# A two-layer transformer kernel with routed experts: token places in two pieces, bf16 ranks, biases joined to the shared sums, maxima split on 128 partitions, down weights quantized later

## The chip, the cores and the metric

The kernel runs on one core of a Trainium2 chip. The metric is the device time of one execution in microseconds (us). A profiled execution is another execution of the same program, recorded by the hardware profiler. In what follows PE is TensorE, DVE is VectorE, ACT is ScalarE, POOL is GpSimd and SP is SyncE, which here does nothing but issue DMAs. L913 is line 913 of the kernel before.

## What is computed

Eight batches (turns) of 512 tokens with 128 features go through two layers, in fp32 unless said otherwise:

```python
xn = layernorm(x)                       # x: (8, 512, 128)
x = x + attn0(xn) + ffn0(xn)            # 16 heads of 8; ffn0: gate, up, down with
                                        # FP4 quantize+dequantize (blocks of 16) of inputs and weights
xn = layernorm(x)
x = x + attn1(xn) + moe(xn)             # attn1 with biases
# moe: logits = relu(xf @ Wr1 + br1) @ Wr2 + br2; top 2 of 8 experts
# out = silu(xf @ Ws1 + bs1) @ Ws2 + bs2                      (shared expert)
# for each e: out += w[:, e] * (silu(xf @ We1[e] + be1[e]) @ We2[e] + be2[e])
```

The softmax of both attentions is taken with the maximum of each row of scores subtracted.

## The kernel before

All of it is written out by hand, engine by engine: five instruction streams (`block.sync`, `gpsimd`, `scalar`, `vector`, `tensor`), each in a fixed order, with semaphores between them. PSUM is divided into three rings. `ring` has two banks and carries every single product or transpose; `sums` (`acc`) has two banks for accumulations; `mx` has two double banks for scores. The order in which names take banks is written in `ring_uses`. An engine that is to reuse a bank waits for the reader of the bank's last content, so a late reader on DVE or ACT holds PE.

Turn `it` has these stages, seen from PE:

- **Scores of layer 0.** For slots k = 1 to 15, four score products (`scores`, L1329) for 4 heads by 128 keys, two exponentials of 128x1024 on ACT (L702), and eight weighted sums (L1321). Beside it DVE normalizes the next batch, quantizes the hidden FFN values (`hidden`), splits q and k of the next batch into three bf16 parts (`split_qk`, L849 to L853; the third part is a POOL subtraction, `third_part`, L527) and quantizes the tokens (`quantize_x`).
- **Scores of layer 1** of the batch before, again 16 slots. In each slot PE also makes two score tiles for the maxima of layer 0 of the next batch (`tile_maxima`, in `ring`; in turn 0 a pair in `mx`), which DVE reduces with a maximum (L917 or L913). Into the slots are set the projection of attention 0, the second normalization, the router, the q and k products of layer 1, and the ranks of the tokens among those that chose the same expert (`ranks`, L1386 to L1390: fp32 products of 0/1 matrices). DVE's `places` turns the ranks into row numbers and POOL's `sort_tokens` scatters the tokens with eight indirect DMAs and loads them back sorted. POOL's order is fixed: `third_part(1, it)`, then `sort_tokens(it)`.
- **The middle.** The shared expert (`shared_hidden`, `shared_out`), the output biases weighted by the router (`output_biases`, in a bank of their own, "mb"), the projection of attention 1, ten places for pairs of maxima, and the gate and up products.
- **The tiles.** 15 tiles of 128 sorted tokens, with expert weights fetched by indirect DMAs, and among them the remaining maxima of layer 0 and all 32 pairs of layer 1 (L913). At tile 4 the row maxima of layer 0 are transposed on PE (`max_rows`), and DVE splits the 16x512 result into two bf16 parts (`split_rows`, L929 and L931), which SP copies into the q stacks as two extra rows. The row maxima of layer 1 follow in the first slots of the next turn; in the last turn at tile 13.

Before turn 0 there is a start: loads, the first normalization, quantization of the FP4 weights in three pieces (gate, up, down; `quantize_weights`), the first q and k split, its stores to DRAM and loads back as stacks (SP, L416 to L430), and the 32 pairs of maxima of batch 0.

DVE's slot order in the second stage before the change (slot_maxima first in each slot) is:

```python
if k == 3: add_projection(0, part, it, it); dve.drain(); norm_stats(1, it)
if k == 4: norm_apply(1, it)
if k == 5 and it > 0: add_experts(it - 1)
if k == 10: split_qk(1, part, it, it); places(part, it)
if k == 11: gate_difference(part, it); sums_out(1, part, it, it - 1, 0)   # the latter if it > 0
```

## Time and profile before

| what | value |
|---|---|
| median of 3 runs | 1478.62 us (1476.63 to 1479.34) |
| the profiled execution | 1480.99 us, of which the span from first to last instruction is 1479.2 us |
| PE matmul busy | 1287.3 us (87%) |
| PE weight load busy | 609.3 us (41%) |
| DVE busy | 1074.9 us (73%) |
| ACT busy | 788.0 us (53%) |
| POOL busy | 401.7 us (27%) |
| mean granted TensorE clock | 0.948 of full |

Turns 1 to 6 are alike, and each takes about 171 to 172 us. The busy shares are averages over stages with different limits, so the stages are read one by one. In a timeline a row is: start in us, length in us, engine, line, operation, what it writes and reads, count, and in brackets the idle time of the engine just before and what ended it. An engine's pieces that follow each other closely are merged.

### The profile page before, as it was taken

The page shows a single profiled execution, that of the slowest core. Times are in us where ns is not written, and L with a number is a line of the kernel's source. Part 1 is how long each engine was busy: PE and PEld are TensorE (multiplying, and loading weights), DVE is VectorE, ACT ScalarE, POOL GpSimd, SP SyncE. Part 2 cuts the span into 40 slices and gives each one's busy share as a digit, 9 for nine tenths or more (in the row PEclk, how much of TensorE's full clock was granted, in tenths as well). Part 3 has the DMA queues.
Part 4 walks back from the last instruction along what each step waited for, and adds up shares of the span by engine and source line. Part 5 has one row for each costly group of instructions (what it writes and reads, how often), then busy time and mean ns, then how long its engine had stood idle before and what let it go on. Part 6 is the DMA issues. An engine that isn't in the chain of part 4 may idle for free.

```text
span 1479.2 us, 22025 instructions
## 1 busy us (share of the span) xinstructions
PE 1287.3 (87%) x7829; PEld 609.3 (41%) x7829; DVE 1074.9 (73%) x1907; ACT 788.0 (53%) x1279; POOL 401.7 (27%) x459
## 2 busy tenths in 40 slices
PE   1578789989999889998899899998899988999886
PEld 1113365334633256233553346332563336433641
DVE  8876789677985689766895779856896679824641
ACT  1145235754477534864357544776348643687355
POOL 6001333114231222314231233313223142303331
PEclk8669599999999999999999999999999999999998
DMA  3303373317514364226533275143642264203730
GB/s 111 100 9 109 119 219 106 99 54 219 161 47 127 96 183 144 86 64 190 150 97 104 65 200 168 40 128 96 192 134 92 58 198 144 90 5 104 223 100 15
DMA packets 120734, 171.76 MB, mean 116 GB/s; under 512 B 18153, under 2 KB 98354, under 8 KB 120626
## 3 DMA queue, kind: packets, MB, share of 16 engines
q0 software_dynamic: 27168, 90.44, 20.2%
q1 hardware_dynamic: 92514, 79.38, 18.3%
q8 instruction: 63, 1.03, 0.3%
q10 hardware_dynamic: 944, 0.54, 0.1%
q14 instruction: 45, 0.37, 0.1%
HBM read 116.88 MB, written 52.89 MB: 115 GB/s over the span
## 4 chain that ended last, share of the span: by engine, by line
PE 53%; DVE 28%; ACT 11%; issue 3%; DVEq 3%; DMA 2%; POOL 0%; ACTq 0%; POOLq 0%
DVE nm L913 19%; PE sums L1321 11%; PE mx L1329 11%; ACT ex L702 9%; PE ring L1211 8%; PE mx L1280 4%; PE ring L1410 3%; PE ring L1217 3%; PE sums L1422 3%; PE ring L1206 3%; PE ring L1280 2%; PE sums L1377 2%; PE ring L1259 2%; PE ring L1399 1%; DVE qk_f L851 1%
## 5 line engine op out<-in xcount | busy, mean ns | idle before, releaser
L702 ACT ACTIVATE ex<-mx 128x1024 f32<-128x1024 f32 x512 | 496.0, 1028 | 178.6 <-PE mx L1329 177.2
L913 DVE TENSOR_REDUCE nm<-mx 128x2 f32<-128x1024 f32 x422 | 490.2, 1215 | 68.1 <-PE mx L1280 68.1
L1329 PE MATMUL mx<-qs,ks 128*128 128x512 bf16 (+1 forms) x1024 | 287.6, 391 | 29.4 <-ACT ex L702 14.9
L715 ACT ACTIVATE ex<-ring,wx_sb 128x128 f32<-128x128 f32 x480 | 136.8, 368 | 222.6 <-PE ring L1410 222.6
L1280 PE MATMUL mx<-ks,qs 64*128 64x512 bf16 x844 | 162.6, 406 | 57.2 <-DVE nm L913 55.5
L1329 PEld LDWEIGHTS mx<-qs,ks 128*128 128x128 bf16 (+1 forms) x1024 | 80.2, 99 | 252.5 <-ACT ex L702 170.8
L552 POOL DMA_INDIRECT wx_sb<-wx,wx_row x120 | 114.6, 955 | 255.0 <-PE sums L1422 240.4
L917 DVE TENSOR_REDUCE nm<-ring 128x1 f32<-128x512 f32 x180 | 115.8, 685 | 62.7 <-PE ring L1280 61.6
L1410 PE MATMUL ring<-xsT,wx_sb 128*128 128x128 f32 x960 | 135.9, 285 | 8.5 <-ACT xsT L656 5.4
L1321 PE MATMUL sums<-ex,vs 128*18 128x512 f32 x1024 | 137.6, 610 | 0.0
L1422 PE MATMUL sums<-wx_sb,ex 128*128 128x128 f32 x960 | 135.6, 284 | 0.0
L1410 PEld LDWEIGHTS ring<-xsT,wx_sb 128*128 128x128 f32 x960 | 118.2, 194 | 25.2 <-issue 22.5
L1422 PEld LDWEIGHTS sums<-wx_sb,ex 128*128 128x128 f32 x960 | 117.0, 191 | 27.1 <-issue 25.9
L527 POOL TENSOR_TENSOR parts<-qk_f,parts 128x512 bf16<-128x512 f32 x32 | 36.3, 1152 | 234.0 <-DVE parts L853 234.0
L1280 PEld LDWEIGHTS mx<-ks,qs 64*128 64x128 bf16 x844 | 37.2, 94 | 151.8 <-DVE nm L913 69.7
L509 POOL TENSOR_TENSOR rstd<-veps,minus_half 128x4 f32<-128x4 f32 x16 | 17.7, 1103 | 260.3 <-DVE veps L835 260.2
L570 POOL DMA_INDIRECT x_sorted<-xn,slot x64 | 62.2, 971 | 63.4 <-DMA x_sorted<-xn,slot 35.4
L600 POOL DMA_INDIRECT xs<-o_sorted,slot x64 | 65.3, 1020 | 35.6 <-DMA xs<-o_sorted,slot 20.4
L1321 PE MATMUL sums<-ex,vs1b 128*18 128x512 f32 x512 | 70.8, 626 | 0.6 <-ACT ex L702 0.6
L1321 PE MATMUL sums<-ex,vs1a 128*18 128x512 f32 x512 | 70.8, 626 | 0.0
L560 POOL DMA_DIRECT2D o_sorted<-xs x32 | 26.1, 814 | 145.4 <-ACT xs L724 107.0
L936 DVE COPY work<-sums 128x512 f32<-128x512 f32 x32 | 22.0, 688 | 55.0 <-PE sums L1321 55.0
(191 smaller groups left out, 1403.0 us busy)
## 6 DMA issues: line engine op xcount, KB each, us to landing
scratch<-parts SPq DMA_DIRECT2D x64, 384.0 KB
ks<-scratch SPq DMA_DIRECT2D x256, 64.0 KB, 2.3
qs<-scratch SPq DMA_DIRECT2D x256, 64.0 KB, 2.2
scratch<-parts SPq DMA_DIRECT2D x32, 256.0 KB
xs<-x_sorted POOLq DMA_DIRECT2D x24, 256.0 KB, 7.5
o_sorted<-xs POOLq DMA_DIRECT2D x24, 256.0 KB, 2.8
rest<-parts SPq DMA_DIRECT2D x32, 128.0 KB
x_sb<-x SPq DMA_DIRECT2D x8, 256.0 KB, 3.3
```

The costliest lines, as they stand in the source:

```text
L552: pool.indirect_dma_start(wx_sb[n % NW][:, :], None, wx, bass.IndirectOffsetOnAxis(ap=wx_row[:, i:i + 1], axis=0)).then_inc(wx_in[n % NW], 16)
L600: pool.indirect_dma_start(moe[:, n, t, :], None, o_sorted, bass.IndirectOffsetOnAxis(ap=slot[it % 2][:, n, t:t + 1], axis=0)).then_inc(moe ...
L702: act.activation(ex[:, ex_buffer(l, b, k), 2 * i:2 * i + 2, :], mx[bank][:, :, :], ACT.Exp, scale=SCALE).then_inc(mx_free[bank], 1)
L715: last = act.activation(ex[:, free_buffer(it, "tiles"), c, i % TG * P:i % TG * P + P], bank[:, c * P:(c + 1) * P], ACT.Silu, bias=wx_sb[n ...
L913: dve.tensor_reduce(nm[l][:, t, h:h + 2], mx[bank][:, :, :], AX.X, ALU.max, negate=True).then_inc(mx_free[bank], 1)
L917: dve.tensor_reduce(nm[0][:, t, h:h + 1], bank[:, :], AX.X, ALU.max, negate=True).then_inc(free, 1)
L1211: pe.matmul(bank[0:rows, 0:width], lhsT, rhs, start=True, stop=True).then_inc(full, 1)
L1280: return pe.matmul(bank, qs[l][r, h, t * P:(t + 1) * P], ks[l][r, h, :], start=True, stop=True)
L1321: last = pe.matmul(acc[bank][32 * j:32 * j + 2 * VW, :], values[:, start:start + 2 * VW], ex[:, ex_buffer(l, b, k), j, :], start=q == 0 an ...
L1329: return pe.matmul(bank, ks[l][r, h, s * P:(s + 1) * P], qs[l][r, h, :], start=True, stop=True)
L1410: last = pe.matmul(bank[:, c * P:(c + 1) * P], wx_sb[n % NW][:, c * P:(c + 1) * P], xsT[:, i // TG % 2, i % TG * P:i % TG * P + P], start= ...
L1422: last = pe.matmul(acc[bank][:, i % TG * P:i % TG * P + P], ex[:, free_buffer(it, "tiles"), c, i % TG * P:i % TG * P + P], wx_sb[n % NW][: ...
```

## The change

- **Order on DVE in the second stage.** The second normalization moves one slot later and now stands behind that slot's maxima (statistics at k = 4, application at k = 5). `places` is cut in two: `first_places` (down to the last reading of the bank with the ranks) at k = 10, the rest at k = 11. `split_qk(1)` moves from k = 10 to k = 12. `sums_out(1, ..., 0)` stands at k = 11, `gate_difference` and `add_experts` at k = 13.
- **Ranks.** `earlier`, `ones` and `choices` are bf16 (0 and 1 are exact).
- **Biases.** The product of router weights and biases is the first term of the accumulation of the shared expert's output. The bank "mb", `add_biases` and its addition on DVE go.
- **Maxima.** DVE splits the 128x4x16 negated maxima into high and low part before the transposes (`split_maxima`: three small operations). PE transposes both, and ACT copies the 32x512 result to bf16. DVE no longer takes part behind the transposes.
- **Start.** The down weights are quantized in the first scores of turn 0, with their transposes on PE and copies on ACT. The first normalization comes before the clearing of the value buffers, and POOL's `set_ones` waits for the normalized tokens (layer 0) and the quantized tokens (layer 1).

```diff
@@ ring_uses
-        r += ["hT0", "hT1", "hT2", "down"]
+        r += ["hT0", "hT1", "hT2"] + ([] if it else ["wd"]) + ["down"]
-        return sums(0) + (sums(1) if it else []) + ["mb", "o"] + [("O", g) for g in range(NTG)]
+        return sums(0) + (sums(1) if it else []) + ["o"] + [("O", g) for g in range(NTG)]
@@ tiles in SBUF
-        earlier, ones = sb("earlier", [P, P]), sb("ones", [P, P])
+        earlier, ones = sb("earlier", [P, P], BF16), sb("ones", [P, P], BF16)
-        nm_hl = sb("nm_hl", [NH, 2, T], BF16)
+        nm_high, nm_parts = sb("nm_high", [P, NT, NH], BF16), sb("nm_parts", [P, NT, 2 * NH])
+        nm_hl = sb("nm_hl", [2 * NH, T], BF16)
@@ gpsimd, start
-            pool.wait_ge(rstd_ready[0], 1)
+            pool.wait_ge(xn_ready[0], 1)
             set_ones(0)
             third_part(0, 0)
-            pool.wait_ge(p3_ready, 1)
+            pool.wait_ge(xq_ready, 1)
             set_ones(1)
@@ scalar
+            def max_rows(l, part, it, b):
...
+                copy_out(part, it, ("m1", b) if l else "m0", nm_hl[:, :], rows=2 * NH)
                 for k in range(LEAD, SLOTS):
+                    if k == 3 and it > 0:
+                        max_rows(1, part, it, it - 1)
...
                     if k == HT_SLOT + 3:
                         ffn_hidden(part, it, (2,))
+                        if it == 0:
+                            down_weights(part, it)
...
                 for i in range(NTILE):
+                    if i == M0_TILE and not last:
+                        max_rows(0, part, it, it + 1)
+                    if i == LAST_M1_TILE and last:
+                        max_rows(1, part, it, it)
@@ vector
-            def split_rows(part, it, name, rows):
...
-                dve.tensor_copy(nm_hl[0:rows, 0, :], bank[0:rows, :])
-                dve.drain()
-                dve.tensor_tensor(nm_hl[0:rows, 1, :], bank[0:rows, :], nm_hl[0:rows, 0, :], ALU.subtract).then_inc(free, 1)
+            def split_maxima(l, first, last):
...
+                n = last - first
+                dve.drain()
+                dve.tensor_copy(nm_high[:, :, 0:n], nm[l][:, :, first:last])
+                dve.drain()
+                dve.tensor_copy(nm_parts[:, :, 0:n], nm_high[:, :, 0:n])
+                dve.tensor_tensor(nm_parts[:, :, n:2 * n], nm[l][:, :, first:last], nm_high[:, :, 0:n], ALU.subtract).then_inc(nm_split, 1)
...
                 if not last:
                     split_qk(0, part, it, it + 1)
+                    if it == 0:
+                        quantize_weights(2)
                     quantize_x(it + 1)
...
                     if k == 3:
                         add_projection(0, part, it, it)
+                    if k == 4:
                         dve.drain()
                         norm_stats(1, it)
-                    if k == 4:
+                    if k == 5:
                         norm_apply(1, it)
-                    if k == 5 and it > 0:
-                        add_experts(it - 1)
...
                     if k == 10:
+                        first_places(part, it)
+                    if k == 11:
+                        places(part, it)
+                        if it > 0:
+                            sums_out(1, part, it, it - 1, 0)
+                    if k == 12:
                         split_qk(1, part, it, it)
-                        places(part, it)
-                    if k == 11:
+                    if k == 13:
                         gate_difference(part, it)
                         if it > 0:
-                            sums_out(1, part, it, it - 1, 0)
+                            add_experts(it - 1)
...
-                add_biases(part, it)
...
                     for l, pair in maxima_of_tile(it, i):
                         maxima(l, part, it, pair)
+                        if pair == NPAIR - 1:
+                            split_maxima(l, 0, NH)
@@ vector, start
-            for values in (vs0, *vs1):
+            norm_stats(0, 0)
+            dve.memset(vs0[:, :, :, :], 0.0)
+            dve.drain()
+            dve.memset(vs0[:, :, :, VW + HD:2 * VW], 1.0)
+            norm_apply(0, 0)
+            for values in vs1:
...
-            quantize_weights(2)
             quantize_x(0)
@@ tensor
             def output_biases(part, it):
                 read_out(pe, part, it, "wT")
-                to_sums(part, it, "mb")
...
-                    last = pe.matmul(acc[bank][:, t * P:(t + 1) * P], w9T[:, t * P:(t + 1) * P], b2_sb[:, :], start=True, stop=True)
-                last.then_inc(mb_done, 1)
+                to_sums(part, it, "o")
             def shared_out(part, it, t):
...
+                pe.matmul(acc[bank][:, t * P:(t + 1) * P], w9T[:, t * P:(t + 1) * P], b2_sb[:, :], start=True, stop=False)
                 for c in range(EC):
...
-                                     start=c == 0, stop=c == EC - 1)
+                                     start=False, stop=c == EC - 1)
```

## Rows read from the trace of the kernel before

**Rows 1.** The page: share of each engine in the chain that ended last.
```profile
PE 53%; DVE 28%; ACT 11%; issue 3%; DVEq 3%; DMA 2%; POOL 0%; ACTq 0%; POOLq 0%
```

**Rows 2.** The waits: who waited for whom, us in total, times, longest.
```profile
PEld ring L1280 <- DVE place L992: 22.3, 6, 3.7
```

**Rows 3.** Timeline of slots 10 to 12 of the second stage, turn 3.
```profile
496.93 0.68 DVE L849 CAST parts<-qk_f 128x1024 bf16<-128x1024 f32 x1
497.29 0.81 PE L1390 MATMUL ring<-choices,ones 128*128 128x24 f32 x6
499.59 0.16 DVE L984 TENSOR_SCALAR padded<-ring 128x8 f32<-128x8 f32 x1
499.83 1.11 DVE L986 TENSOR_SCALAR padded<-padded 128x8 f32<-128x8 f32 x1
501.01 1.09 DVE L988 TENSOR_TENSOR binade<-below,padded 128x64 f32<-128x64 f32 x1
...
502.73 0.60 PE L1280 MATMUL ring<-ks,qs 64*128 64x512 bf16 x1 [3.42 <-DVE place L992]
502.92 0.19 DVE L996 TENSOR_TENSOR place_b<-place,chosen 128x32 f32<-128x32 f32 x1
...
504.38 1.28 DVE L917 TENSOR_REDUCE nm<-ring 128x1 f32<-128x512 f32 x2
505.58 0.18 DVE L1011 TENSOR_REDUCE gsum<-le 128x4 f32<-128x32 f32 x1
507.07 1.28 DVE L917 TENSOR_REDUCE nm<-ring 128x1 f32<-128x512 f32 x2
```

**Rows 4.** Windows: us, busy time of PE, PEld, DVE, ACT, POOL, granted clock, DMA.
```profile
503.00:507.00 4.00, 4.00 (x19) 0.82 (x22) 3.56 (x16) 0.76 (x1) 1.93 (x2) 0.61 1.01 335
```

**Rows 5.** Timeline of slots 4 to 6 of the second stage, turn 3.
```profile
474.45 1.28 DVE L917 TENSOR_REDUCE nm<-ring 128x1 f32<-128x512 f32 x2
475.19 1.16 PE L1217 MATMUL ring<-wqkv_sb,xnT 128*128 128x128 f32 x8 [0.87 <-DVE nm L917]
...
478.95 2.35 DVE L1056 SCALAR_TENSOR_TENSOR macc<-xs,tg,macc 128x128 f32<-128x128 f32 x8
...
482.23 0.63 PE L1206 MATMUL ring<-ident,xn 128*128 128x128 f32 x4 [1.41 <-DVE nm L917]
```

**Rows 6.** Timeline of tile 4, turn 3.
```profile
551.77 0.67 DVE L929 CAST nm_hl<-ring 16x512 bf16<-16x512 f32 x1
...
553.12 9.13 DVE L913 TENSOR_REDUCE nm<-mx 128x2 f32<-128x1024 f32 x8
...
554.47 0.39 PE L1280 MATMUL mx<-ks,qs 64*128 64x512 bf16 x2 [0.75 <-DVE nm L913]
```

**Rows 7.** Timeline of the scores of layer 0, turn 4, ACT.
```profile
605.78 0.59 ACT L656 COPY xnT<-ring 128x512 f32<-128x512 f32 x1
```

**Rows 8.** Timeline of the start.
```profile
8.91 3.86 DVE L841 TENSOR_SCALAR xn<-x_sb,mv,rstd 128x128 f32<-128x128 f32 x4 [1.24 <-POOL rstd L509]
...
30.87 0.85 PE L1568 MATMUL ring<-ident,work 128*128 128x128 f32 x3 [10.46 <-DVE work L891]
...
33.79 0.54 SPq L426 DMA_DIRECT2D ks<-scratch  x1
...
43.76 1.12 PE L1206 MATMUL ring<-ident,xq 128*128 128x128 f32 x4 [4.89 <-DVE xq L891]
```

**Rows 9.** Timeline of turn 0, end of the scores of layer 0.
```profile
134.36 0.69 DVE L906 TENSOR_TENSOR acc<-acc,ring 128x512 f32<-128x512 f32 x1 [8.34 <-PE ring L1259]
```

**Rows 10.** Timeline: first transposes of sorted tokens in turn 3, then the last turn.
```profile
537.38 0.66 PE L1399 MATMUL ring<-ident,xs 128*128 128x128 f32 x4
...
1347.56 2.28 POOL L527 TENSOR_TENSOR parts<-qk_f,parts 128x512 bf16<-128x512 f32 x2 [15.67 <-DVE parts L853]
...
1352.59 1.05 POOL L570 DMA_INDIRECT x_sorted<-xn,slot  x1 [2.75 <-DVE slot L1007]
...
1374.42 0.66 PE L1399 MATMUL ring<-ident,xs 128*128 128x128 f32 x4 [2.88 <-DMA xs<-x_sorted]
```

More of the change, by code:

```diff
@@ L724, in tiles_out, with down_weights @@
                 act.copy(xs[:, tiles.start:tiles.stop, :].rearrange("p i c -> p (i c)"), acc[bank][:, 0:len(tiles) * P]).then_inc(acc_free[bank], 1)
+            def down_weights(part, it):
+                bank, free = from_ring(part, it, "wd")
+                act.copy(wdT[:, 0:2, :], bank[:, 0:2 * P].rearrange("p (c n) -> p c n", c=2))
+                act.copy(wdT[0:FC[2][1], 2, :], bank[0:FC[2][1], 2 * P:3 * P]).then_inc(free, 1)
             def turn(it, part):
@@ L800, in _ @@
                 copy_out("ahead", 0, name, dst[:, :], width=F0)
-            bank, free = from_ring("ahead", 0, "wd")
-            act.copy(wdT[:, 0:2, :], bank[:, 0:2 * P].rearrange("p (c n) -> p c n", c=2))
-            act.copy(wdT[0:FC[2][1], 2, :], bank[0:FC[2][1], 2 * P:3 * P]).then_inc(free, 1)
             copy_out("ahead", 0, "xqT", xqT[:, :])
@@ L1252, in ffn_hidden, with down_weights @@
                     transpose_tiles(part, it, f"hT{c}", lambda t: h_sb[:, t, f:f + n], cols=n)
+            def down_weights(part, it):
+                pe.wait_ge(fp4_done, 3)
+                bank, full = to_ring(part, it, "wd")
+                for c, (f, n) in enumerate(FC):
+                    last = pe.transpose(bank[0:n, c * P:(c + 1) * P], work[:, 6 * P + f:6 * P + f + n], ident[:, :])
+                last.then_inc(full, 1)
             def ffn_down(part, it, b):
-                read_out(pe, part, it, "hT2")
+                read_out(pe, part, it, "hT2" if it else "wd")
                 bank, full = to_ring(part, it, "down")
@@ L1569, in _ @@
                 last.then_inc(full, 1)
-            pe.wait_ge(fp4_done, 3)
-            bank, full = to_ring("ahead", 0, "wd")
-            for c, (f, n) in enumerate(FC):
-                last = pe.transpose(bank[0:n, c * P:(c + 1) * P], work[:, 6 * P + f:6 * P + f + n], ident[:, :])
-            last.then_inc(full, 1)
             quantized_x("ahead", 0, 0)
```

77 lines of the change are left out of this document (34 added, 43 removed).

## The prediction

> **What bounds the kernel now.** I began with the chain that ended last [rows 1]: PE has just over half of it and DVE most of the rest, so no engine alone sets the time; it goes back and forth between PE and DVE. The list of waits then says where PE stands still for DVE in one place: 22.3 us in six waits of up to 3.7 us, for the reading of the bank with the ranks, L992 [rows 2]. The timeline around it [rows 3] shows why. PE has made the ranks, but DVE first splits q and k (496.93 to 499.59) and then needs 3.33 us more until L996. Two tiny operations in it, L986 and L988, take 1.11 and 1.09 us while POOL subtracts the third part; neighbours of their size take 0.2 us. PE's second maxima tile of slot 11 needs the bank and waits 3.42 us. After it the granted clock is 0.61 over 4 us [rows 4], that is, much of the stretch runs at the lower of the two levels (1.2, not 2.4 GHz); at half speed its work costs some 1.5 us more. So this place costs about 4.9 us in each of turns 1 to 6. Smaller ones: PE waits for DVE in slots 4 and 6 [rows 5] and in the tiles [rows 6]. The start and the last turn are read separately, since other things end last there [rows 8, 10].
>
> **Slots 10 to 15, turns 1 to 6.** I write a new DVE schedule in the old turn's clock times, with distances from start to start in rows 3: the split 2.66 us, a slot's pair of maxima 1.20 (504.38 to 505.58), second piece of the places 1.46 (502.92 to 504.38), gate difference with the sums' copy 1.49 (505.58 to 507.07), and `add_experts` 2.44 (its row of 2.35 and a drain, rows 5). The first piece took 3.33; beside an idle POOL its two slow operations should have a distance of 0.25 instead of 1.18 each, so 1.48.
> The ranks ended at 498.10. In fp32 each product leaves twice as many records as in bf16 (x6 for three products at L1390, x2 for two at L1280), so I take half of the 1.5 us for the six products: 0.75 less. The bounds are 0 and 1.5.
> DVE then: ranks 497.35, first piece to 498.8, maxima 500.0, second piece 501.5, sums 502.1, maxima 503.3, split 506.0, maxima 507.2. POOL's third part now runs from 506.1 to 508.4 [2.28, rows 10]. The gate difference has two-input operations like L988, so I let it wait for POOL's end: 0.9 + 0.7, to 508.8. `add_experts` to 511.2, maxima of slots 14 and 15 to 513.6, before 515.1. PE's first shared product follows PE's last tile; before it came at 514.7, now at about 513.8.
> So the long wait goes, but only 0.9 us of the 4.9 come back. What is late next is DVE itself: it now has 16 us of work on end in slots whose scores and exponentials PE and ACT do in 2.3 us each, and PE will wait for maxima in slots 14 and 15 instead. Bounds 0.2 (more overlap lost) and 1.6 (no waiting for POOL, no rank cost).
> The Trainium skill (GPSIMD Engine Reference, Specifications) says that POOL's SBUF interfaces are shared with VectorE and that DVE instructions with two SBUF inputs or in a two-port mode collide with it. L986 and L988 agree, 1.1 for 0.2 us. It speaks against one edit, since `add_experts`, which reads two SBUF tensors, now comes close behind the third part; by that rule nothing else changes in my sum, and without it the sum would be 0.7 us a turn better.
>
> **Slots 3 to 7, turns 1 to 6.** The normalization's statistics (1.5 us on DVE) now stand behind the maxima of slot 4, so the bank for v of layer 0 is free 0.87 us earlier [rows 5]. `add_experts` no longer stands in front of the maxima of slot 6: their first reduction, which released PE at 482.23, moves from 481.39 to about 479.7. For this the application of the normalization, which now stands between the maxima of slots 5 and 6, must be done at 479.7; by my schedule it is, with nothing to spare. PE's transposes: 482.23 to 480.5. Gain 1.75 us, with the 0.87 in it. Bounds 0.9 and 2.2.
>
> **Tiles, turns 0 to 6.** The split behind the transposes took DVE 1.35 us (551.77 to 553.12) [rows 6], after which DVE's maxima ran 9.13 us without a pause and PE waited 0.75 for them. The three small operations with drains come to some 0.7 us, by the second piece of the places (ten operations in four drained steps, 1.46). Gain 0.65 a turn. ACT's copy lies in the tiles beside idle time. Bounds 0 and 0.75.
>
> **Scores of layer 0, turns 1 to 7.** ACT gets the copy of layer 1's row maxima, 0.59 us [rows 7], where exponentials fill nearly every moment; PE's transposes were there before. Following PE and ACT for two slots, half of it remains: +0.3 a turn. Bounds 0 and 0.6. What DVE saves here is hidden by its own later waits.
>
> **Biases, bank "mb".** The same eight weight loads and products, only in another bank; DVE loses an addition of 0.7 us where it waits for PE. Nothing, within 0.3 either way.
>
> **Sum for a turn 1 to 6:** -0.9 - 1.75 - 0.65 + 0.3 = -3.0; six turns -18.0.
>
> **The start.** Before, the normalization took 3.86 us beside POOL's clearing [rows 8]; alone some 1.1. But DVE waits for x first and clears two buffers later, so the FP4 weights begin only 0.6 us earlier, and with them the first split, the stores and the stack loads: 33.8 becomes 33.2. Between the up weights (30.87) and the quantized tokens (43.76) lay two quantizations, the down weights and the tokens; without one, and with POOL's clearing out of the way, the tokens are done by 36. Then the stacks are late: the first four loads are issued at 0.64 us each and land 2.2 us later, at 37.9. The first maxima can start there and not at 44.8: -6.9. The two old splits (1.35 each) become 0.7 on DVE, but the second stands now in front of PE's last transposes, where the old one stood behind: -1.3 + 0.7 = -0.6. Sum -7.5. Bounds -4 (loads held up by other transfers) and -9.
>
> **Turn 0.** The down weights cost DVE 4.5 us beside its idle 8.34 [rows 9], PE 0.85 and ACT 0.6, which I put at +1. In the second stage I get -0.7: the same order frees DVE by about 2.2, but the normalization behind the maxima costs 1.5, since here PE waits for it. With the tiles: -0.4.
>
> **The last turn.** There are no maxima of a next batch, so PE waits for the sorted tokens: 2.88 us at 1374.42 [rows 10]. `sort_tokens` stands behind `third_part` in POOL's queue. Before, the third part began at 1347.56, ahead of the places, and the scatter at 1352.59. Now the order is ranks 1346.4, first piece 1347.9, second 1349.4, sums 1350.0, split 1352.7, third part 1355.0, scatter 1355.5: 2.9 later, and all behind it. +2.9, and +0.3 for ACT. SP's queue is moved too: stores and stack loads begin 5.4 us later and run longer into the tiles, beside the weight fetches. I put that at nothing, with 2 us either way. At tile 13, the early split and ACT's copy against DVE's two operations: even.
>
> **Total:** -18.0 - 7.5 - 0.4 + 3.2 = -22.7. The profiled execution has 1480.99, so 1458.3; the median is 2.4 lower than that execution, so 1455.9. I say 1456.
>
> **Rivals.**
> A. *DVE keeps up.* The wait and the low clock go without a successor. For it: DVE was idle about 1 us a slot from slot 12 on. Against it: 16 us of work. It gives 4.9 + 0.75 instead of 0.9, so 4.75 more in six turns: 1427.
> B. *The clock falls in the new waits.* PE will stand still some 4 us of the 8 in slots 13 to 15, in pieces of 0.5 to 2.4. For it: the 3.42 us wait brought the clock down [rows 4]. Against it: after the wait in slot 6 four transposes took 0.63 us as always. A stretch like that of rows 4 in each turn costs 1.5 to 2 us: +10, 1466. The Trainium skill (TensorE: Matmul & The Clock Gate, "A second HAM failure mode: psum-queue depth-cycling") tells of a kernel whose frequent short pauses let the clock alternate; no run here shows that yet.
> C. *The edits cancel.* DVE's order yields nothing, since `add_experts` between maxima costs what its old place cost, and the start is held by the loads: -18 becomes about -2, -7.5 becomes -4: 1475.
> D. *Slower: the sorted tokens come late in every turn.* In the last turn the way from first scatter to first transposes is 21.8 us [rows 10]. In turn 3 the places were done at 504.4 [rows 3] and the scatter followed at 504.8, so tokens were there near 526.6 and wanted at 537.38: 10.8 to spare. The new order takes 4.8 of it (scatter 3.9 later, PE 0.9 earlier). From 6 us more on it costs time in seven turns, and from 9.2 more on the gain of 22.7 is gone; at 10.5 more, 1487. Against it: the same DMAs, with the same neighbours.
>
> **Chances.** The forecast 0.58, with its own range 1446 to 1464 (the bounds above do not all fall one way); B 0.22; A 0.08; C 0.07; D 0.05. The range 1441 to 1470 takes in the forecast and B. 0.2% is 3 us, about what a measurement of this kernel can tell from no change. Faster 0.91, same 0.03, slower 0.06.
>
> **What would show it.** L986 and L988 near 0.2 us; no wait for L992 above 0.5 us; PE waits for L917 of 1 to 2.5 us in slots 14 and 15 of turns 1 to 6; `add_experts` after the split. First maxima at about 38 us. In the last turn a scatter 3 us later relative to the ranks, and a longer wait for sorted tokens. It is wrong if these new waits are missing (A), if the clock after them is below 1 (B), if the transposes of sorted tokens wait in turns 1 to 6 (D), or if the start gains less than 4 us.

## The result, and the profile of the changed kernel

| what | before | changed |
|---|---|---|
| median of 9 runs | 1479.34 us (1476.22 to 1481.10) | 1471.51 us (1464.26 to 1475.19) |
| profiled execution, span | 1480.99, 1479.2 us | 1464.26, 1462.5 us |
| ratio to before | | 0.9942, 95% interval 0.9924 to 0.9960 |

So 7.8 us faster (0.6%), where 22.7 were forecast; the time lies 1.5 us above the range. The profiled execution of the changed kernel was the fastest of its nine.

The times of one PE event after another give the length of each stage. (The rows ahead of the prediction count the turns from one: their "turn 3" has it = 2. From here on, turn n is the one with it = n.) "Again" is a second profiled execution of the changed kernel, "start only" the kernel before with the new start (experiments 1 and 5 below). Each column is one execution; experiments 13 to 15 give one more of each of the three kernels, and there turns 1 to 6 repeat to 2.2 us or better, while the other stages differ by up to 4.3.

| stage, us | before | changed | again | start only | predicted step |
|---|---|---|---|---|---|
| to the first down product | 131.4 | 120.8 | 125.1 | 123.4 | -6.5 |
| turn 0, from down product to down product | 153.9 | 156.5 | 157.5 | 150.8 | -1.4 |
| turns 1 to 6 | 1027.9 | 1019.6 | 1019.6 | 1028.8 | -18.0 |
| the rest | 166.0 | 165.7 | 165.9 | 163.3 | +3.2 |
| span | 1479.2 | 1462.5 | 1468.1 | 1466.3 | -22.7 |

And the mean of turns 1 to 6, by stage: down product to router 27.8, now 26.0 (predicted -1.75, measured -1.8); router to ranks 11.7 in both; ranks to first shared product 18.7, now 17.7 (predicted -0.9, measured -1.0); **the middle, first shared product to first transposes of sorted tokens, 22.7, now 24.9 (predicted 0, measured +2.1)**; tiles and next scores -0.7 (predicted -0.35). The gain is lost in the middle, in turn 0, and in that the usual execution of the changed kernel is slower than the profiled one.

The page of the changed kernel, share of each engine in the chain that ended last, for [rows 1]. PE gave 6 points, and DMA, 2% before, has 4%:

```profile
PE 47%; DVE 29%; ACT 10%; DMA 4%; issue 4%; DVEq 3%; POOL 1%; SPq 1%; ACTq 0%; POOLq 0%
```

The waits of the changed kernel (who waited for whom: us in total, times, longest). The wait of [rows 2] is gone (22.3 us before PE's weight loads, 20.5 before its products), and 22.7 us before products stand in its place, now for the maxima. PE also waits for sorted tokens in two turns, not one:

```profile
PE ring L1311 <- DVE nm L947: 22.7, 24, 2.7
PE ring L1423 <- DMA xs<-x_sorted: 8.6, 2, 5.7
```

The timeline of slots 10 to 15 in turn 2, changed kernel, for [rows 3] (start, length, engine, line, operation, in brackets the idle time before):

```profile
486.87 0.22 PE L1414 MATMUL ring<-choices,ones 128*128 128x24 bf16 x3
...
487.36 0.17 DVE L1011 TENSOR_SCALAR padded<-padded 128x8 f32<-128x8 f32 x1
487.61 0.23 DVE L1013 TENSOR_TENSOR binade<-below,padded 128x64 f32<-128x64 f32 x1
...
488.46 0.39 PE L1311 MATMUL ring<-ks,qs 64*128 64x512 bf16 x1 [0.18 <-DVE place L1017]
...
493.14 0.69 DVE L879 CAST parts<-qk_f 128x1024 bf16<-128x1024 f32 x1
...
495.97 2.27 POOL L536 TENSOR_TENSOR parts<-qk_f,parts 128x512 bf16<-128x512 f32 x2 [23.38 <-DVE parts L883]
...
497.51 0.76 DVE L1042 TENSOR_TENSOR gpair<-le,gsum 128x8 f32<-128x8 f32 x1
...
498.61 2.35 DVE L1078 SCALAR_TENSOR_TENSOR macc<-xs,tg,macc 128x128 f32<-128x128 f32 x8
...
501.05 2.48 DVE L947 TENSOR_REDUCE nm<-ring 128x1 f32<-128x512 f32 x4
...
501.80 0.39 PE L1311 MATMUL ring<-ks,qs 64*128 64x512 bf16 x1 [2.31 <-DVE nm L947]
```

The wait for the bank of the ranks is 0.18 us, but DVE has work without a pause from 493.1 to 503.5. PE's first maxima tile of slot 14 waits 0.93 us. Its first tile of slot 15 waits 2.31 us: the bank it needs comes free only when DVE, through with the routed sum (L1078), has reduced the first maxima of slot 14. This second wait is there in each of turns 1 to 6 (2.31 to 2.67 us).

Windows of the changed kernel behind that wait, turns 1, 2 and 3 (us; busy time of PE, PEld, DVE, ACT, POOL; granted clock; DMA share, GB/s):

```profile
331.00:339.00 8.00, 8.00 (x29) 1.91 (x29) 2.84 (x9) 2.66 (x3) 4.60 (x5) 0.62 0.70 220
502.80:510.80 8.00, 7.35 (x36) 2.48 (x36) 5.48 (x14) 3.02 (x4) 4.98 (x6) 1.00 0.73 228
671.40:679.40 8.00, 7.77 (x33) 2.17 (x33) 4.07 (x11) 2.66 (x3) 3.85 (x5) 0.79 0.71 228
```

The granted clock falls to its lower level (0.5 of full, 1.2 GHz) at the head of the middle in five of the six turns, for 6.8 us in turn 1 and for 3.4 us in turns 3 to 6. Turn 2, where it stays up, has 40.8 us from ranks to sorted tokens; the others have 42.6 to 43.8, together 10.6 us more. In the kernel before, the low stretch lay in slots 11 to 13 of all six turns [rows 4] and the middle was at full clock in each of them. That low stretch is 3.4 us long in turns 2 (the one of [rows 4]) and 5, but 6.8 us in the other four.

The other places: the start, turn 0 (the normalization in slot 6, then sorted tokens) and the last turn, for [rows 8] and [rows 10]:

```profile
36.58 1.03 PE L1311 MATMUL mx<-ks,qs 64*128 64x512 bf16 x4 [2.18 <-DMA qs<-scratch]
137.88 1.12 PE L1229 MATMUL ring<-ident,xn 128*128 128x128 f32 x4 [4.11 <-DVE xn L871]
183.62 1.11 PE L1423 MATMUL ring<-ident,xs 128*128 128x128 f32 x4 [2.93 <-DMA xs<-x_sorted]
...
1338.54 1.05 POOL L579 DMA_INDIRECT x_sorted<-xn,slot  x1 [0.18 <-issue]
...
1361.08 1.12 PE L1423 MATMUL ring<-ident,xs 128*128 128x128 f32 x4 [5.69 <-DMA xs<-x_sorted]
```

### The profile page after: what moved, and what is told of

Its sections match the earlier page's. It is cut to its first block, busy times and chain, and to the rows that moved or that the text cites. A ratio compares the mean times of both kernels' runs of the same rounds, so it can differ in the third digit from the quotient of the medians.

```text
span 1462.5 us, 21919 instructions
## 1 busy us (share of the span) xinstructions
PE 1278.2 (87%) x7743; PEld 603.3 (41%) x7781; DVE 1041.2 (71%) x1916; ACT 797.1 (55%) x1296; POOL 399.9 (27%) x459
## 4 chain that ended last, share of the span: by engine, by line
PE 47%; DVE 29%; ACT 10%; DMA 4%; issue 4%; DVEq 3%; POOL 1%; SPq 1%; ACTq 0%; POOLq 0%
DVE nm L943 19%; PE sums L1349 9%; ACT ex L711 8%; PE mx L1357 8%; PE ring L1234 7%; PE ring L1434 4%; PE mx L1311 4%; PE sums L1446 3%; PE ring L1229 3%; DVE nm L947 3%; PE ring L1240 3%; PE sums L1401 2%; DMA x_sorted<-xn,slot 2%; PE ring L1290 1%; PE ring L1311 1%
## 5 line engine op out<-in xcount | busy, mean ns | idle before, releaser
L1357 PE MATMUL mx<-qs,ks 74*128 74x512 bf16 (+1 forms) x986 | 273.5, 384 | 33.3 <-ACT ex L711 15.6
L1446 PEld LDWEIGHTS sums<-wx_sb,ex 128*128 128x128 f32 x960 | 117.3, 192 | 26.5 <-issue 25.3
L1311 PE MATMUL ring<-ks,qs 64*128 64x512 bf16 x180 | 46.5, 388 | 24.4 <-DVE nm L947 22.7
```

Of the source, the lines that this page charges most:

```text
L1311: return pe.matmul(bank, qs[l][r, h, t * P:(t + 1) * P], ks[l][r, h, :], start=True, stop=True)
L1357: return pe.matmul(bank, ks[l][r, h, s * P:(s + 1) * P], qs[l][r, h, :], start=True, stop=True)
L1446: last = pe.matmul(acc[bank][:, i % TG * P:i % TG * P + P], ex[:, free_buffer(it, "tiles"), c, i % TG * P:i % TG * P + P], wx_sb[n % NW][: ...
```

## The experiments

Theory to be tested: the start gives the whole net gain, and what the new order on DVE gives in turns 1 to 6 is paid back by three things that the sum had at nothing: the order of the bias products, the clock behind the new wait, and late sorted tokens in turn 0. Ratios are to the kernel before in the same rounds. Stages come from one profiled execution of each kernel.

**1. The changed kernel again.**

> The changed kernel once more, nothing edited, on the chip and in the rounds of the next three. Theory K (the clock): its executions differ by how often PE's clock falls behind the waits for DVE in slots 13 and 14 of the second stage. The execution profiled first had 1464 us and clock 0.957, the median one 1471.5 us and 0.950. This theory expects a time of 1464 to 1475, and in a profile of a slower execution more or longer stretches at a granted clock near 0.5 between slot 13 and the first shared products, the rest of the turn unchanged. Rival (transfers vary from run to run): the same time with the same low stretches, the difference then lies in waits for DMAs.

1470.54 us (before 1477.02; ratio 0.9957, 0.9945 to 0.9968). The profiled execution is 5.6 us longer than the first one, and the theory had the wrong place: turns 1 to 6 agree to 0.1 us in sum, low stretches included. The difference lies in the first 150 us (first ranks at 152.6, not 147.6). Windows of the first and of this execution, in this order, across the first scores:

```profile
80.00:96.00 16.00, 14.27 (x68) 2.99 (x68) 8.20 (x29) 13.05 (x14) 1.03 (x1) 0.75 0.07 19
```
```profile
80.00:96.00 16.00, 14.23 (x46) 2.65 (x44) 7.39 (x27) 9.89 (x11) 1.03 (x1) 0.50 0.07 19
```

The clock, which has been low since the maxima of the start, came back at 88 us in the first and only at 97 us in the second. So the clock explains most of it, but not at the place that the theory named. The rival (waits for DMAs) has a small part: PE waits 10.3 us for sorted tokens, not 8.6, and turn 0 is 1.0 us longer.

**2. Biases in one block.**

```diff
 output_biases:
+    for t in range(NT):
+        pe.matmul(acc[bank][:, t * P:(t + 1) * P], w9T[:, t * P:(t + 1) * P], b2_sb[:, :], start=t == 0, stop=False)
 shared_out:
-    pe.matmul(acc[bank][:, t * P:(t + 1) * P], w9T[:, t * P:(t + 1) * P], b2_sb[:, :], start=True, stop=False)
...
-                                     start=False, stop=c == EC - 1)
+                                     start=False, stop=t == NT - 1 and c == EC - 1)
```

> The changed kernel with the four products of the biases in one block in front of the shared expert's products, all sixteen and these in one accumulation group; the same weight loads and products as before, in another order. Theory S (switching): PE pays for going back and forth between weights of 9 rows and of 128 rows. In the changed kernel the stretch from the biases to the last shared product takes 6.0 us of PE's time, in the kernel before 5.04. This theory expects 0.9 to 1.1 us less in each of turns 1 to 6 between first shared product and first transposes of sorted tokens, nothing in turn 0 and the last turn where sorted tokens are waited for: 6 us less than the changed kernel of the same rounds, about 1465. Rival (the place is bound by something else, so the order does nothing): 1471, and the stretch stays at 6.0 us.

1467.40 us (1460.18 to 1476.61; ratio 0.9941, 0.9916 to 0.9965): 3 us less than the changed kernel where 6 were expected, with single executions spread over 16 us, so the time by itself decides nothing. In the profiled execution the clock fell in all six turns, not in five, and turns 1 to 6 gained only 1.5 us. The stage itself is clear: in turn 1, with the same low stretch, the middle went from 25.8 to 24.7 us. Groups by line (busy us, mean ns), first of the changed kernel, then with the block:

```profile
L1401 PE MATMUL sums<-w_sb,ex 128*128 128x128 f32 x256 | 37.1, 288 | 0.0
L1399 PE MATMUL sums<-b_sb,r_sb 9*128 9x128 f32 x64 | 15.5, 321 | 0.3 <-ACT r_sb L665 0.3
```
```profile
L1403 PE MATMUL sums<-w_sb,ex 128*128 128x128 f32 x256 | 32.1, 279 | 0.0
L1392 PE MATMUL sums<-b_sb,r_sb 9*128 9x128 f32 x64 | 9.2, 283 | 0.3 <-ACT r_sb L665 0.3
```

The same 320 records are busy for 52.6 us when the two kinds alternate and for 41.3 us when they don't (in eight turns, partly overlapping). The single records of turn 2 show where it goes: within one kind they start 0.11 us apart, but the distance across a change of kind and the next one after it are 0.20 to 0.21 us each. The changed kernel has seven changes of kind a turn, the block one. Six changes at 0.19 us are 1.15 us. The edit also joins four accumulation groups into one, but that is not the cause: the kernel before has separate groups, no alternation, and the same means of 279 and 283 ns. Theory S holds. That it is the number of rows in the weights, and not another difference between the two kinds, no run isolates.

**3. The routed sum in the scores of layer 0.**

```diff
                 sums_out(0, part, it, it, 0)
+                if it > 0:
+                    add_experts(it - 1)
                 ffn_down(part, it, it)
...
                     if k == 13:
                         gate_difference(part, it)
-                        if it > 0:
-                            add_experts(it - 1)
```

> The changed kernel with the routed sum (eight additions on DVE, 2.44 us) in the scores of layer 0, where DVE waits 8.3 us for PE in each turn, and no longer in slot 13 of the second stage. Theory K: its place in slot 13 causes PE's wait of 2.3 to 2.8 us for the maxima of slot 14, and this wait lets the clock fall. It expects the wait below 1 us, a granted clock of 1.0 in the middle stage of every turn, 1.2 to 2 us a turn less from ranks to first shared product, 0.6 to 1.9 less behind it, together 12 to 18 us: 1453 to 1460, and a smaller spread of the runs. Rival D2 (DVE stays too late without it, since split and maxima alone fill slots 12 to 14): a gain of 0 to 5 us, and the low stretches stay.

1443.73 us (1441.42 to 1449.58; ratio 0.9785, 0.9767 to 0.9804): 26.8 us less than the changed kernel, half as much again as the upper end. The long wait is gone, not halved, and no low stretch is left in turns 1 to 6. Ranks to first shared product takes 14.4 us instead of 17.7, the middle 23.9 instead of 24.9. From ranks to sorted tokens that is 2.6 us in turn 2, where the clock had stayed up, and 4.2 to 5.6 us in the five others. Waits, and windows behind slot 15 in turns 1 and 2:

```profile
PE ring L1311 <- DVE nm L947: 7.0, 13, 0.9
```
```profile
331.40:339.40 8.00, 7.34 (x38) 3.19 (x32) 5.91 (x9) 4.72 (x7) 4.62 (x5) 1.00 0.72 225
497.40:505.40 8.00, 7.34 (x36) 3.19 (x32) 5.95 (x9) 4.68 (x7) 5.01 (x6) 1.00 0.71 227
```

The middle at full clock keeps 1.2 us over the kernel before: that is the biases.

**4. Three scatters ahead of the third part.**

```diff
+                scatter_tokens(it, 0, FIRST_SCATTERS)
                 third_part(1, it)
                 sort_tokens(it)
```

`FIRST_SCATTERS` is 3, and `sort_tokens` now begins with the fourth scatter (its code is left out here).

> The changed kernel with the first three scatters of the tokens ahead of the third part of q and k in POOL's queue. Theory T (sorted tokens): in turn 0 PE waits 2.9 us and in the last turn 5.7 us for sorted tokens, because the scatter stands behind the third part and this behind the later split. It expects sorted tokens 4 to 5 us earlier in every turn: turn 0 loses its wait of 2.9 and up to 3 us of the low clock behind it, the last turn gains 4, turns 1 to 6 nothing: 8 to 10 us less than the changed kernel, about 1462. Rival (the scatters are bound by the queue of DMAs and by stores beside them, so an earlier start moves their end little): less than 3 us.

1464.24 us (1460.47 to 1471.52; ratio 0.9920, 0.9900 to 0.9939), 6.3 less than the changed kernel, where 8 to 10 were expected. The scatter begins 5 us behind the ranks, not 12. Turn 0 takes 150.8 us, not 157.5 (experiment 1): its wait for sorted tokens and the low stretch behind it are gone. In the last turn the wait falls from 6.2 us (5.7 in the first execution) to 2.2:

```profile
PE ring L1430 <- DMA xs<-x_sorted: 2.2, 1, 2.2
```

Turns 1 to 6 have 1019.9 us, unchanged. The theory holds for turn 0. In the last turn almost nothing of the shorter wait reached the time: the stage behind the last down product has 165.5 us instead of 165.9, with two low stretches of the clock behind 1400 us that experiment 1 doesn't have.

**5. The start alone**, in the kernel before (first normalization, clearing, down weights).

```diff
+            norm_stats(0, 0)
+            dve.memset(vs0[:, :, :, :], 0.0)
...
+            norm_apply(0, 0)
...
             quantize_weights(1)
-            quantize_weights(2)
...
-            pool.wait_ge(rstd_ready[0], 1)
+            pool.wait_ge(xn_ready[0], 1)
```

> The kernel before with the start of the changed kernel alone: first normalization ahead of the clearing of two value buffers, clearing of the stacks behind the normalized and the quantized tokens, down weights quantized in the first scores. Theory A1: the start gives nearly the whole gain of the change (6.5 us of the medians in these rounds), and what the other parts give in turns 1 to 6 (8.3 us in the profiled executions) they lose again in turn 0 and in the low clock. It expects first maxima at 36 to 37 us instead of 44.8, 8 us less up to the first down product, and no change behind it: 1477 becomes 1467 to 1470. Rival A2: the first scores take the gain back, since the down weights' quantization stands in DVE's queue there: 0 to 4 us less.

1467.71 us (1466.91 to 1469.95), before 1477.11; ratio 0.9940, 0.9926 to 0.9953. The first maxima begin at 36.64 us:

```profile
36.64 1.03 PE L1296 MATMUL mx<-ks,qs 64*128 64x512 bf16 x4 [2.19 <-DMA qs<-scratch]
```

In later rounds with all three kernels side by side (13 to 15 below) start only has 1466.70 (1465.66 to 1468.44), the changed kernel 1470.83 (1464.96 to 1473.05). The start is worth more than the whole change: the other edits together cost some 4 us by the medians (2.8 by the means of six and nine executions, which overlap). Theory A1 holds.

**6. The routed sum moved in the kernel before**, from slot 5 to the same place as in 3.

```diff
-                    if k == 5 and it > 0:
-                        add_experts(it - 1)
```

> The kernel before with one edit: the routed sum moves from slot 5 of the second stage to the scores of layer 0, beside DVE's wait for PE. Theory P (price by place): DVE's 2.44 us cost 1.4 us in slot 5 (PE's wait in front of the four transposes of slot 6) and cost more in slot 13, where DVE has no idle time left; moved out of both, old and new kernel gain what the place cost. It expects 1.4 us a turn, 8 us in all: 1477 becomes 1467 to 1470. Rival: slot 5 was hidden by other waits (PE then waits for the normalization instead), so less than 3 us; then the changed kernel's move into slot 13 has cost its whole 27 us.

1469.55 us (ratio 0.9949, 0.9936 to 0.9963), 7.6 less. Down product to router goes from 27.8 to 26.4 us a turn: the wait of 1.41 in [rows 5] is gone. 0.4 of it comes back behind the ranks, so turns 1 to 6 go from 1027.9 to 1021.5 us. The same 2.4 us of DVE work cost 1.1 us a turn in slot 5 and 4.3 in slot 13 (1019.6 against 993.9 in run 3; 2.6 in the turn whose clock stayed up). Beside DVE's 8.3 us wait they cost nothing that can be seen: the stage from sorted tokens to the next down product keeps its 90.4 us in the kernel before and its 89.7 in the changed one.

**7. fp32 ranks, on top of 3.**

```diff
-earlier, ones = sb("earlier", [P, P], BF16), sb("ones", [P, P], BF16)
+earlier, ones = sb("earlier", [P, P]), sb("ones", [P, P])
...
-chosen, choices = sb("chosen", [P, 2, NT, NX]), sb("choices", [P, NT, NX], BF16)
+chosen, choices = sb("chosen", [P, 2, NT, NX]), sb("choices", [P, NT, NX])
```

> The changed kernel with the routed sum in the scores of layer 0 (1443.7 us in the rounds before) and the ranks in fp32 again (twice the records on PE). It prices the bf16 ranks where the clock stays up. Theory R: PE's ranks end 0.75 us later, DVE's first piece of the places with them, and PE waits that much longer: 0.7 to 1.5 us a turn, 5 to 10 us slower than with bf16. Rival: the ranks are hidden between maxima that DVE releases later anyway: within 2 us.

1457.06 us (1451.28 to 1459.47; ratio 0.9855, 0.9836 to 0.9874), 13.3 more than with bf16 in other rounds (the kernel before had 1477.1 and 1477.0 in the two), and more than the 5 to 10 expected. Ranks to first shared product 15.6 us instead of 14.4, that is 1.2 a turn, 7 us in turns 1 to 6; the rest is the start, whose clock came back late in this execution (first ranks at 152.8, not 148.5 us), and the last turn (174.3, not 168.9 us behind the last down product). bf16 is worth 1.2 us a turn, not the 0.75 of the prediction: the first rank product to DVE's first reading took 1.54 us in fp32 and 0.34 in bf16.

**8. Edits 2, 3 and 4 together**, and in turn 0 the second normalization at its old place (statistics in slot 3, application in slot 4).

> The changed kernel with four edits: routed sum in the scores of layer 0, biases in one block, three scatters ahead of the third part, and in turn 0 the second normalization where it was before (PE waited 4.1 us for it there, 1.3 us in the kernel before). If the causes are separate they add up: 1443.7 us for the first, 6 us less for the biases (1.1 us a turn was seen in the turn with the same clock), 5 us in turn 0 and 4 us in the last turn for the scatters, 2 to 3 us for the normalization in turn 0: 1425 to 1431. Rival (each hides behind the next, PE then waits for the exponentials or for DVE's maxima): 1436 to 1442.

**1426.19 us (1423.52 to 1429.97), ratio 0.9665, 0.9647 to 0.9683**: 51 us faster than the kernel before, 44 than the changed one, and within the range of the theory that the parts add up. The middle has 22.7 us again, in every turn but one (23.0), turn 0 150.4, turns 1 to 6 987.5. Only turn 0 gains little on run 4 (150.8), though two more of the edits touch it. PE's wait for the normalization there is 1.26 us again. What is left of the last turn's wait:

```profile
PE ring L1432 <- DMA xs<-x_sorted: 4.4, 1, 4.4
```

**9. The routed sum in two halves**, in slots 13 and 14 of the changed kernel.

```diff
-                            add_experts(it - 1)
+                            add_experts(it - 1, (0,))
+                    if k == 14 and it > 0:
+                        add_experts(it - 1, (1,))
...
```

The body of `add_experts`, which takes the half as an argument, is left out.

> The changed kernel with the routed sum cut in two: its first four additions in slot 13, the other four in slot 14 behind that slot's maxima. DVE's work in slots 10 to 15 is the same. Theory K1 (what lets the clock fall is one long wait of PE, 2.3 to 2.8 us in slot 14, not the share of idle time): the wait is cut to some 1.1 us in each of two slots, the granted clock stays at 1.0 in most turns, the stages behind gain 0.6 to 1.9 us a turn, and the time falls 4 to 8 us below the changed kernel's 1470.5. Rival K2 (idle time as such, in whatever pieces): the same sum of waits, the same stretches at half clock, within 2 us of 1470.5.

1463.97 us, but in these rounds the kernel before had 1526.97 us, not 1477 (more on this at 13 to 15), and the changed kernel was not among them; only stages are compared. The wait of 2.31 us in slot 15 became one of 1.09 (1.44 in turn 6), and 0.64 in front of the first shared product:

```profile
502.55 0.39 PE L1315 MATMUL ring<-ks,qs 64*128 64x512 bf16 x1 [1.09 <-DVE nm L947]
...
505.16 1.13 PE L1238 MATMUL ring<-xnT,w_sb 128*128 128x512 f32 x2 [0.64 <-DVE nm L947]
```

Ranks to first shared product 16.5 us, not 17.7, with the same work on DVE. The middle was at full clock in four turns (23.9 us) and at 25.3 in turns 4 and 5, whose waits are no longer than those of turns 1 to 3. So the same work cut in pieces lets the clock stay up oftener, not always. K1 and K2 are not separated by it: K2 presumed the same sum of waits, and PE's waits for the maxima also fell in sum, from 3.8 to 3.0 us a turn.

**10 and 12. All eight scatters first (`FIRST_SCATTERS` is 8), and 11. the kernel of 8 beside it**, again in rounds with a slow kernel before.

> The kernel with the four edits (1426.2 us) and now all eight scatters of the tokens ahead of the third part, not three. Theory T: in the last turn PE still waits for sorted tokens (3 us or so more than in the kernel before), and in every turn the third part has room, since its stacks are read only in the tiles. It expects tokens 2 to 3 us earlier, the last turn 2 to 3 us shorter, and nothing else: 1423 to 1425. Rival T2: the third part then starts some 8 us later, stores and stack loads move into the middle and the first tiles, collide with the weight fetches, and PE waits for stacks in the tiles: slower by 3 us or more in all turns.

> The kernel with the four edits once more, so that it and the next one have the same chip (in the last rounds the kernel before itself had 1527 us, not 1477). If the chip is the one of the earlier rounds: 1424 to 1430. On the chip of the last rounds all kernels with many transfers may be slower; the gain of the four edits against the kernel before should then be at least as large, 50 us or more.

> All eight scatters ahead of the third part once more, beside the kernel with three of them on the same chip. Its trace showed 17 waits of PE for expert weights in the tiles, 13 us in all (2 of them, 1.9 us, with three scatters), which speaks for rival T2: stack loads that begin some 8 us later run beside the weight fetches. Theory T2 expects 5 to 15 us more than with three scatters. Theory T (those waits came from the chip, not from the order) expects 0 to 3 us less.

1448.19 (before 1526.97) and 1448.76 us with eight scatters; 1434.40 (1431.29 to 1438.32) with three, in the rounds of 1448.76, before 1524.85. Eight are 14 us slower, as T2 has it. The last turn's tokens do come earlier (its middle 18.0, not 18.5 us), but PE then waits 7.1 us in one place of the last turn for the stacks of q, and in the tiles for expert weights. Of the 18.8 us between the two profiled executions 11.6 lie behind the last down product and 5.6 in turns 1 to 6, so the "in all turns" of T2 is the smaller part. The waits of run 12 (the other 2.2 us for q are in the start of every run with the new start):

```profile
PE mx L1318 <- DMA qs<-scratch: 9.3, 2, 7.1
PE ring L1443 <- DMA wx_sb<-wx,wx_row: 5.0, 9, 1.0
```

**13 to 15. Before, changed and start only, side by side.**

> The kernel before, unchanged. On one chip it takes 1477 us, on another 1525, while the kernel with four edits takes 1426 and 1434. On the second chip, theory X1 (transfers land later there, and the kernel before has a place where a transfer is needed just in time) expects waits of PE for DMAs that the first profile does not have, some 7 us a turn in turns 1 to 6, at one place. Theory X2 (the granted clock is lower there) expects the same waits and more stretches at 0.5; the executions' mean clock there was 0.930 to 0.946 against 0.948. On the first chip: 1477 and nothing new.

> The changed kernel, unchanged, on the same chip as the one above. On the second chip: if the place that costs the kernel before 48 us is one that the change has touched, 1470 to 1480, that is a gain of 45 us or more; if not, 1515. On the first chip 1470.

> The kernel before with the start of the changed kernel, on the same chip. The start lies outside turns 1 to 6, so on the second chip it should gain its 9 us and no more: 1516. If it falls to 1470 to 1480, the 48 us lie in the start or in turn 0.

1477.83, 1470.83 (ratio 0.9948, 0.9928 to 0.9969) and 1466.70 us (0.9932, 0.9912 to 0.9952). This repeats the result. The stages of these three profiled executions:

| stage, us | before | changed | start only |
|---|---|---|---|
| to the first down product | 128.6 | 121.2 | 122.9 |
| turn 0 | 158.1 | 156.1 | 152.9 |
| turns 1 to 6 | 1028.1 | 1019.5 | 1026.6 |
| the rest | 163.6 | 169.0 | 163.0 |

The start and turn 0 trade with each other from execution to execution (131.4 and 153.9 us, then 128.6 and 158.1, in the same kernel before), so they are best taken together.

Why the kernel before takes 48 us more in the rounds of 9 to 12, while that of 8 takes 8 more, stays open: no trace of it was taken there. The expectations of 11 and 13 call it another chip, but that isn't shown: a chip numbered 11 stands both at experiments 1 to 4, with 1477.02 us, and at 11 and 12, with 1524.85. The kernel before also had a lower granted clock there (mean of an execution 0.930 to 0.946, against 0.944 to 0.956 in the rounds of 13 to 15).

## Why the prediction was right in sign and wrong in size

- **The wait for L992: right.** Two tiny operations went from 1.11 and 1.09 us [rows 3] to 0.17 and 0.23, the wait from 3.42 to 0.18. The successor was named too: PE waits of 0.9 to 1.3 us in slot 14 and 2.3 to 2.7 in slot 15 (1 to 2.5 were forecast). Slots 10 to 15 gave -1.0 us a turn, -0.9 were predicted, and that they agree is luck: the bf16 ranks gave 1.2 us, not 0.75, while the low clock took some 0.8 back (turn 2, without it, has 16.9 us here, the mean is 17.7).
- **Slots 3 to 7: right** (-1.8 for -1.75 us a turn). Tiles and scores of layer 0 gave -0.7 for -0.35; no run separates the split that went from the copy that came to ACT.
- **"Biases: nothing, within 0.3 either way": the step that failed in the arithmetic.** It took the products to be the same and only the bank another, and did not look at their order. 9-row and 128-row products alternate now, which costs 1.1 us a turn (runs 2 and 8), 6.6 us in turns 1 to 6.
- **The clock behind the new waits, at nothing in the forecast: the step that failed in the mechanism.** Rival B, with a chance of 0.22, came true in mechanism and price: +10 predicted, 10.6 measured, in five of six turns. The prediction held against it that the wait in slot 6 had done nothing to the clock; but that one is 1.4 us long, the new one 2.3 to 2.7, nearer to the 3.4 that stood before the low stretch in the kernel before. Run 3 shows it, since the low stretches go with the wait: the six long waits (14.3 us) and the 10.6 us are together 24.9 of the 25.7 us that it gains in turns 1 to 6. The price itself was partly luck: [rows 4] is one of the two turns with a low stretch of 3.4 us, four have 6.8.
- **Turn 0, "-0.4": failed.** Against the start alone (150.8 and 152.9 us in two executions) the changed kernel has 156.1 to 157.5 in three, so the other edits cost 3 to 7 us here. The prediction had set the normalization at +1.5; PE's wait for it rose by 2.8 (1.31 to 4.11). And rival D was worked out for turns 1 to 6 and for the last turn, not for turn 0, whose second stage is shorter: tokens came 2.9 us late there, and a low clock followed. Run 4 gives 6.7 us back. In turns 1 to 6 D did not happen: no PE wait for tokens, though the scatter is 3.5 to 3.7 us later behind the ranks (3.9 predicted).
- **The start: right, and better than said.** First maxima -8.2 us, -6.9 predicted. It alone yields 9.4 and 10.5 us by the medians of two sets of rounds. Start and turn 0 together were forecast at -7.9 us, and the change gave -8.0 in the first execution (277.3 for 285.3 us), then 282.6 and 277.3 against 286.7: two errors that cancel, a better start and a worse turn 0.
- **The last turn: right for the wait.** For sorted tokens it is +2.8 (+2.9 predicted) in the first executions, 2.9 to 5.7 us, and 2.3 to 6.2 in the second ones. The scatter is 2.3 us later behind the ranks, not 2.9. The first stage table shows nothing of it (166.0 and 165.7 us for +3.2 predicted), since low stretches of the clock differ from execution to execution there; against start only it is +2.4 to +6.0.
- **From profile to median.** The prediction took 2.4 us off the profiled execution. Here the profiled one was 7.3 us below the median, which is 9.7 of the 15.6 us between forecast and result. Part of it is the start, where the clock came back 9 us earlier than in experiment 1 (5.6 us of time). But in experiment 14 it came back as early, and the execution had 1467.7 us with a longer last turn. Why the median is where it is stays open.

Sum for turns 1 to 6: -18.0 predicted; +6.6 for the biases, +6.0 for the clock in the middle (2.1 less 1.1, six times; its other 4.6 us are inside the next term), -0.6 in slots 10 to 15, -2.4 in slots 3 to 7 and the tiles: -8.4, measured -8.3.

The whole, forecast to result: +9.7 us in turns 1 to 6, +4.0 in turn 0, -4.1 up to the first down product, -3.6 behind the last one, +9.7 from profile to median. That is the 15.6 us by which the result is above 1455.9, and without the last term the time would have been inside the range.

## What to carry to other kernels

Ask of each piece of work not how long it takes but where the engine has to wait anyway: the same 2.4 us of DVE work cost 4.3, 1.1 or 0 us a turn, depending on its place, and some 1.7 of the 4.3 were the clock behind the wait. When a long wait is removed, price its successor with the clock behind it, and treat the first and last turn as kernels of their own. Undo the edits of a bundle one by one: here one part was worth more than the whole. Profile a kernel more than once before reading a stage that differs by 3 us.

## What the runs showed of the hardware

- Alternating fp32 products with 9 and with 128 weight rows costs PE 1.1 us a turn more than one block of 8 and two of 16: 321 ns mean for a 9-row record against 283 in a block, 288 against 279 for the others. Start to start, two neighbouring records are 0.11 us apart within a kind, and each change of kind adds 0.19 us (runs 2 and 3).
- DVE operations with two SBUF inputs slow down beside POOL's subtraction. L1013 now runs alone, L1042 now runs beside the third part; groups by line, changed kernel, then kernel before:

```profile
L1042 DVE TENSOR_TENSOR gpair<-le,gsum 128x8 f32<-128x8 f32 x8 | 6.2, 775 | 0.6
L1013 DVE TENSOR_TENSOR binade<-below,padded 128x64 f32<-128x64 f32 x8 | 1.8, 225 | 0.6
```
```profile
L988 DVE TENSOR_TENSOR binade<-below,padded 128x64 f32<-128x64 f32 x8 | 8.7, 1090 | 0.6
L1015 DVE TENSOR_TENSOR gpair<-le,gsum 128x8 f32<-128x8 f32 x8 | 1.7, 215 | 0.9 <-issue 0.4
```

  The collision moved with the order, from 1090 to 225 ns in the one and from 215 to 775 in the other. This agrees with the Trainium skill (GPSIMD Engine Reference, Specifications), which has such DVE instructions contend with POOL for the SBUF interfaces. Two inputs are not the only case: the tensor_scalar on 128x8, with one, took 1.11 us beside POOL [rows 3] and 0.17 alone, while a reduction and a reciprocal of 128x4 took 0.18 us beside it in the changed kernel.
- Behind a wait of 2.3 us the granted clock fell to 0.5 in five of six turns, behind two of 1.1 and 0.6 us (run 9) in two of six, and behind 0.9 us alone (runs 3 and 8) in none. The same wait at the same place does not always do it: turn 2 kept full clock in three executions of the changed kernel, and lost it in runs 2 and 4, and in run 4 turn 4 kept it. The Trainium skill (TensorE: Matmul & The Clock Gate, "A second HAM failure mode: psum-queue depth-cycling") tells of a clock that alternates because of frequent short pauses; the traces here agree that it alternates, but the longer pause did it oftener than the shorter ones.
- In the start, the clock came back at 88, 88 and 97 us in three executions of the changed kernel (first ranks at 147.6, 147.7 and 152.6 us), and at 103 and 95 us in two of the kernel before. What decides between them is open.
- The kernel before had medians of 1477 us in three sets of rounds and of 1525 and 1527 in two others, the kernel of run 8 1426 and 1434. What makes the difference is open, so a ratio holds for the rounds in which it was measured.
